# Two layers of attention and experts: for the first sequence only the two chosen experts of a token are computed, in gathered blocks, and in causal heads TensorE does the steps between heads in the middle of a batch

## The reference

```
logits = xf @ Wr + br
topk_w, topk_idx = top_k(logits, 2)
topk_w = softmax(topk_w)
gate = sum(one_hot(topk_idx, 8) * topk_w[..., None], axis=1)
h = relu(einsum('th,ehf->etf', xf, W1) + b1)        # 128 -> 256
y = einsum('etf,efh->eth', h, W2) + b2              # 256 -> 128
out = einsum('te,eth->th', gate, y)
```

## Time and profile before

| | |
|---|---|
| median of 3 runs | 1223.13 us (1223.12 to 1223.13) |
| profiled execution, its own time | 1223.02 us |
| its span, first to last instruction | 1221.2 us |
| TensorE / VectorE / ScalarE / GpSimd busy | 91% / 71% / 64% / 23% |
| heads of layer 0 | to 307.5 us |
| experts 0 | 307.5 to 446.6 us |
| heads of layers 1 and 2 | 446.6 to 1089.4 us |
| experts 1 | 1089.4 to 1211 us |

### The profile page before, as it was taken

The page is one execution under the profiler, slowest core; times in us unless marked ns, Lnnn a source line. Parts: engine busy times, 40 slices in busy tenths (PEclk is TensorE's granted clock), DMA queues, the critical chain, the costliest instruction groups (busy, mean ns, idle before and its releaser), DMA issues. The chain is left out here.

```text
span 1221.2 us, 24980 instructions
## 1 busy us (share of the span) xinstructions
PE 1105.6 (91%) x8797; PEld 605.1 (50%) x8872; DVE 864.5 (71%) x2072; ACT 777.3 (64%) x1569; POOL 281.8 (23%) x824
## 2 busy tenths in 40 slices
PE   5899998999999989999988999788888988899996
PEld 3466676655776755666655642222112221137774
DVE  3788767784334467888776889899999989904433
ACT  4366656667444426677666658878888878874443
POOL 8134322333102113433332431111101010100001
PEclk9799999999999999999999999999999989999998
DMA  3444343110000801243312221101111100000000
GB/s 88 118 115 109 96 96 87 49 31 12 1 1 1 184 10 32 59 105 94 85 49 65 55 43 36 24 16 24 36 36 36 23 11 16 7 1 1 10 9 18
DMA packets 40058, 57.71 MB, mean 47 GB/s; under 512 B 9494, under 2 KB 15078, under 8 KB 39678
## 3 DMA queue, kind: packets, MB, share of 16 engines
q1 hardware_dynamic: 39934, 56.11, 18.8%
HBM read 30.81 MB, written 24.64 MB: 45 GB/s over the span
## 5 line engine op out<-in xcount | busy, mean ns | idle before, releaser
L851 ACT ACTIVATE probs<-bank 128x512 f32<-128x512 f32 x1088 | 574.9, 601 | 240.8 <-PE bank L1210 239.8
L950 DVE TENSOR_REDUCE tile_max<-bank 128x1 f32<-128x512 f32 (+3 forms) x1152 | 611.9, 592 | 40.2 <-PE bank L1195 35.6
L1195 PE MATMUL bank<-qk 125*128 125x128 bf16 (+2 forms) x1664 | 389.1, 312 | 66.8 <-DVE tile_max L950 47.0
L1210 PE MATMUL bank<-qk 128*128 128x128 bf16 (+4 forms) x1608 | 362.6, 305 | 5.7 <-ACT probs L851 5.3
L1239 PE MATMUL bank<-probs,v_head 128*32 128x512 f32 (+3 forms) x3328 | 302.9, 453 | 0.1
L1195 PEld LDWEIGHTS bank<-qk 125*128 125x128 bf16 (+1 forms) x1664 | 132.4, 97 | 313.7 <-DVE tile_max L950 243.0
L1117 DVE SCALAR_TENSOR_TENSOR acc<-bank,gate,acc 128x128 f32<-128x128 f32 x256 | 71.9, 343 | 156.7 <-PE bank L1372 156.7
L1239 PEld LDWEIGHTS bank<-probs,v_head 128*32 128x32 f32 x3328 | 139.6, 109 | 52.7 <-issue 29.8
L1210 PEld LDWEIGHTS bank<-qk 128*128 128x128 bf16 (+1 forms) x1664 | 133.1, 97 | 57.2 <-ACT probs L851 21.0
L871 ACT ACTIVATE probs<-bank,sb_b 128x512 f32<-128x512 f32 x128 | 81.0, 684 | 117.9 <-PE bank L1361 117.9
L944 DVE TENSOR_REDUCE tile_max<-bank 128x4 f32<-128x512 f32 x128 | 87.4, 687 | 90.0 <-PE bank L1195 89.9
(11 more groups left out here) (132 smaller groups left out, 664.2 us busy)
## 6 DMA issues: line engine op xcount, KB each, us to landing
qk<-qk_parts SPq DMA_DIRECT2D x160, 144.0 KB
qk_parts<-q_parts SPq DMA_DIRECT2D x48, 192.0 KB, 2.4
qk_parts<-k_parts SPq DMA_DIRECT2D x48, 192.0 KB, 3.2
qk_parts<-q_parts SPq DMA_DIRECT2D x24, 96.0 KB, 2.3
qk_parts<-k_parts SPq DMA_DIRECT2D x24, 96.0 KB, 2.9
sb_w<-in_w SPq DMA_DIRECT2D x8, 256.0 KB, 3.6
sb_w<-in_w SPq DMA_DIRECT2D x2, 1024.0 KB, 5.2
qk<-neg_rows SPq DMA_DIRECT2D x96, 6.0 KB
```

The source lines that it names most:

```text
L851: nc.scalar.activation(probs[:, hd.probs_place(c), :], S2[i % len(S2)][:], ACT.Exp, scale=hd.a.scale).then_inc(sem("probs"), 1)
L950: ins = nc.vector.tensor_reduce(tile_max[:, hd.slot, t, which:which + 1], s1[:, at:at + P * count], AX.X, ALU.max)
L1195: ins = mm(s1[:, at:at + P * count], qk[hd.query_rows, hd.place, 0, P * t:P * (t + 1)], qk[hd.query_rows, hd.place, 1, P * k0:P * (k0 + co ...
L1210: ins = mm(s2[:, at:at + P * count], qk[hd.key_rows, hd.place, 1, P * j:P * (j + 1)], qk[hd.key_rows, hd.place, 0, P * q0:P * (q0 + count) ...
```

## The change

For sequence 0 of each mixture, once routing has picked two experts for each token, every pair of token and expert gets a slot in a list that is sorted by expert, where each expert begins on a multiple of 128. There are at most 23 blocks of 128 slots (`BLOCKS`). GpSimd writes each token's row to its two slots in DRAM (`x_blocks`, 16 indirect DMAs of 128 rows, step `scatter`), SP loads the blocks back (`blocks`), TensorE turns them (step `gx`, VectorE copies to `xgT`), and six block units of up to four blocks (`BLOCK_UNITS`) take the place of 16 dense ones: `UNITS` is 22, of which the last 16 are the dense units of sequence 1. Since the expert of a block is only known on the chip, SP reads it to a register and loads the block's weights, 256 KB, from `w_blocks`, where DMAs have put W1 and W2 of an expert side by side. 14 or 18 blocks are loaded in the last heads, to memory that is free there (weights of the other stretch, parts of sequence 0, `a_tok`, `x_plus`), the rest at the end. ScalarE makes `hidden` block by block, since the bias differs. VectorE copies `Y` out, SP stores it to `y_blocks`, GpSimd gathers each token's two rows (16 indirect DMAs, step `gather`), and VectorE adds them with their weights (step `combine`).

Four places (`IN_FRONT`) stand ahead of `up(0)` of a stretch. The gate sums (`gateT`, `gb`) of sequence 0 move from the heads into the stretch. In causal heads TensorE now does a place's steps behind the second chunk of the next batch, as in non-causal ones, and ScalarE and VectorE read a chunk later. The beginning has nine more small instructions of GpSimd for constants.

```diff
+BLOCKS = (TOP * S + E * (P - 1)) // P
+BLOCK_UNITS = -(-BLOCKS // TPC)
+PRELOADED = 18
+UNITS = BLOCK_UNITS + CB * E
+IN_FRONT = 4
...
+first = at_unit(0, -1, 0)
+put(first, ("biases", 0))
+for m, i in enumerate((0, 1, 5, 7, 9, 11)):
+    put(later(first, i), ("gx", 0, m))
+put_attention_out(0, 1, first, (2, 3, 4, 6, 8, 9, 10, 12, 13, 14))
+put_routing(0, 1, first, (14, 15, 15, 16, 16))
+put_gate_sums(0, 1, first, (17, 18, 26, 27))
+put_gate_sums(0, 0, first, (19, 20, 21, 22))
+for c, i in enumerate((24, 29)):
+    put(later(first, 17), ("gather", 0, c))
+    put(later(first, i), ("combine", 0, c))
...
+            def blocks(f):
+                sp.wait_ge(sem("scattered"), 16 * TOP * TB * (f + 1))
+                for m in range(BLOCK_UNITS):
+                    n = len(blocks_of(m))
+                    sp.dma_start(xg[m][:, 0:P * n].rearrange("p (j d) -> p j d", d=D),
+                                 x_blocks[f].rearrange("(j p) d -> p j d", p=P)[:, TPC * m:TPC * m + n, :]
+                                 ).then_inc(sem(f"x_in{m}"), 16)
+                for j in range(PRELOADS[f][0], PRELOADED, 4):
+                    preload(f, range(j, min(j + 4, PRELOADED)))
+                sp.wait_ge(sem("pv"), BATCHES[RUNS[f].stop])
+                load_block_weights(f, range(PRELOADED, BLOCKS))
...
+            def scatter(f, i):
+
+                t = i % TB
+                pool.wait_ge(sem("slots"), f + 1)
+                pool.wait_ge(sem("cleared"), 16 * BLOCKS * (f + 1))
+                if f == 1:
+                    taken(pool, "mtok", t // TPC)
+                tokens_of = (x, x_plus)[f]
+                nc.gpsimd.indirect_dma_start(x_blocks[f], bass.IndirectOffsetOnAxis(ap=places[:, i:i + 1], axis=0),
+                                             tokens_of[:, t, :], None).then_inc(sem("scattered"), 16)
+
+            def gather(f, c):
+
+                pool.wait_ge(sem("pv"), BATCHES[RUNS[f].stop])
+                for m in range(2):
+                    pool.wait_ge(sem(f"y_stored{m}"), 16 * BLOCK_UNITS // 2 * (f + 1))
...
             def experts(f, last):
+                normalise(last)
+                for i in range(IN_FRONT):
+                    between(at_unit(f, -1, i))
+                dve.wait_ge(sem("out"), last + 1)
...
-                        if c == batch[1] and before is not None and not HEADS[before[1]].a.causal:
+                        if c == batch[1] and before is not None:
                             between(before)
...
-                    if hd.a.causal:
-                        between(at_head(g, k))
...
                 loaded(pe, f"ffn{f}")
                 pe.wait_ge(sem("max_taken"), CHUNKS[RUNS[f].stop])
+                turn_sums(last)
+                for i in range(IN_FRONT):
+                    between(at_unit(f, -1, i))
                 up(0)
-                turn_sums(last)
```

More of the change, by code:

```diff
@@ L206, in put_attention_out, with put_routing, put_gate_sums, put_places_of_tokens @@
     return at[9]
-def put_routing(f, b, place, at=range(9)):
-    c0, c1 = BY_SEQUENCE[b]
-    for i, step in zip(at, (("logits", f, b), ("route_top", f, b), ("route_exp", f, b), ("route_weights", f, b),
-                            ("route_gate", f, b), ("gateT", f, c0), ("gateT", f, c1), ("gb", f, c0), ("gb", f, c1))):
-        put(later(place, i), step)
+def put_routing(f, b, place, at):
+    for i, step in zip(at, ("logits", "route_top", "route_exp", "route_weights", "route_gate")):
+        put(later(place, i), (step, f, b))
+def put_gate_sums(f, b, place, at=range(4)):
+    for i, step in zip(at, [(kind, f, c) for c in BY_SEQUENCE[b] for kind in ("gateT", "gb")]):
+        put(later(place, i), step)
+def put_places_of_tokens(f, place, at, each):
+    for i, step in zip(at, ("ranks", "slots", "blocks")):
+        put(later(place, i), (step, f))
+    for i in range(TOP * TB):
+        put(later(place, at[1] + 1 + int(i / each)), ("scatter", f, i))
 def put_qkv(L, c, place, offsets=range(4)):
@@ L373, in build @@
         gateT = aT[0:E, :]
+        zeros = sb("zeros", [P, D])
+        weighted = sb("weighted", [P, TOP, TB, E])
+        chosen = sb("chosen", [P, TB + 1, E], BF16)
+        ranks = sb("ranks", [P, TB + 1, E])
+        counted = sb("counted", [P, 5, E])
+        tables = sb("tables", [P, BLOCKS, E])
+        block_at_i = sb("block_at_i", [P, BLOCKS], I32)
+        block_at = sb("block_at", [P, BLOCKS])
+        expert = sb("expert", [P, BLOCKS])
+        expert_i = sb("expert_i", [P, BLOCKS], I32)
+        b1_blocks = sb("b1_blocks", [P, FB, BLOCKS])
+        places_f = sb("places_f", [P, TOP, TB])
+        places = sb("places", [P, TOP * TB], U32)
+        earlier16 = sb("earlier16", [P, P], BF16)
+        ones16 = sb("ones16", [P, P], BF16)
+        before128 = sb("before128", [P, E, E])
+        xg = [part[:, i, S:T].bitcast(F32) for part in parts for i in range(PARTS)]
+        xgT = [rest[:, i, :] for i in range(2)]
+        y_out = sums
+        yg = probs[:, 4:8, :].rearrange("p a (t d) -> p (a t) d", d=D)
         iota_i = sb("iota_i", [P, E], I32)
@@ L644, in between @@
                         route_gate(*which)
+                    if kind == "scatter":
+                        scatter(*which)
+                    if kind == "gather":
+                        gather(*which)
             def route_gate(f, b):
@@ L731, in _ @@
                 add_quarters(GROUP[run.stop - 1])
-                for m in range(UNITS):
-                    for half in range(2):
-                        between(at_unit(f, m, half))
+                between(later(at_unit(f, -1, 0), -1))
+                for place in units_places(f):
+                    between(place)
         @block.scalar
@@ L790, in between @@
                         nc.scalar.activation(xT[:, tokens(which[1])], SHARED[:], ACT.Copy).then_inc(sem("taken"), 1)
+                    if kind == "mtok":
+                        full(act, step)
+                        nc.scalar.activation(x_plus[:, tiles(which[0]), :],
+                                             SHARED[:].rearrange("p (t d) -> p t d", d=D), ACT.Copy
+                                             ).then_inc(sem("taken"), 1)
                     if kind == "eff":
@@ L853, in head @@
                         before = at_place_before(run, g, k)
-                        if c == batch[hd.read_after] and before is not None:
+                        if c == batch[2] and before is not None:
                             between(before)
@@ new lines, in combine @@
+            def combine(f, c):
+                dve.wait_ge(sem(f"gathered{c}"), 16 * TOP * TPC * (f + 1))
+                taken(dve, "gb", f, c)
+                for i in range(TOP):
+                    for t in range(TPC * c, TPC * (c + 1)):
+                        ins = nc.vector.scalar_tensor_tensor(acc[:, t, :], yg[:, TB * i + t, :], small[:, 1 + i, t:t + 1],
+                                                             acc[:, t, :], ALU.mult, ALU.add)
+                    if i == 0:
+                        link(ins)
+                ins.then_inc(sem("combined"), 1)
@@ L1092, in between @@
                         route_weights(*which)
+                    if kind == "ranks":
+                        take_ranks(step)
+                    if kind == "blocks":
+                        block_of(*which)
+                    if kind == "slots":
+                        slots(*which)
+                    if kind == "biases":
+                        biases(*which)
+                    if kind == "combine":
+                        combine(*which)
+                    if kind == "gx":
+                        f, m = which
+                        n = P * len(blocks_of(m))
+                        full(dve, step)
+                        if m >= 2:
+                            dve.wait_ge(sem("hid_ps"), UNITS * f + m - 1)
+                        nc.vector.tensor_copy(xgT[m % 2][:, 0:n], SHARED[:, 0:n]).then_inc(sem("taken"), 1)
                     if kind == "v":
```

300 lines of the change are left out of this document (245 added, 55 removed).

## The result

The changed kernel took 1243.64 us (median of 4 runs, 1238.71 to 1246.69) where the kernel before took 1223.13: a ratio of 1.0163, with an interval of 1.0126 to 1.0200. In these runs it is slower, by 1.3 to 2.0%, and my prediction of 1196 us (1178 to 1214) was wrong.

What follows compares the result with a forecast made beforehand. TensorE was taken to bound the expert stretches, VectorE the non-causal heads. Terms: -66.1 + 9.7 + 24.0 + 3.0 + 4.0 + 1.0 - 3.0 = -27.4 us, giving 1196 us, range 1178 to 1214.

Steps and rivals of the forecast that it cites:

- the pricing of GpSimd's indirect DMAs: Scatters and gathers: GpSimd's time for one bounded by 0.3 and 1.28 us times two, taken as 1.2.
- the rival on the slower side: Gathers behind units 6 to 12, scatters in layer 0's heads: slow indirect DMAs make the change end slower; chance 0.10.
- The lock: In the stretches, GpSimd locked while VectorE adds gathered rows: 16 instructions of 0.34 us, 5.5 a stretch; chance 0.05.
- the rival *between: Gathers of 1.3 to 1.8 us, or GpSimd locked during VectorE's adds: 1207 us, with both up to 1220; chance 0.13.
- the causal order: Causal heads: TensorE's step moves behind the next batch's second chunk, some waits go, others grow; -3.0 us, bounds -12 and +3.
- the half clock: Behind each front, some 4.6 us at the lower clock of 1.2 GHz, so 2.3 us lost at each.
- The saving of work: Expert stretches: 16 dense units go, 23 blocks and their transposes come; -33.0 us a stretch, -66.1 in all.
- the fronts: Ahead of `up(0)`: first waits for GpSimd's last scatter and the load, second for VectorE's biases; +24.0 us with half clock.
- The waits for turned tokens: At `gx` 2 to 5, `up` waits for VectorE's copies: 1.2 us idle, four times a stretch, +9.7 us in all.
- The heads: Heads outside the stretches: VectorE's bookkeeping +4.0 us in layer 2 and +1.0 in layer 0, causal order -3.0.
- the 4.0 of my sum: Layer 2's heads, where VectorE idles 2.6%: its new bookkeeping of 17 instructions makes them +4.0 us longer.
- Loads of weights: Last heads: the 18 and 14 early weight loads stay hidden, priced at nothing; otherwise 3.6 us in a head.

Runs made afterwards that it cites:

- the execution with the delay: Profile of the changed kernel as first run, when ScalarE and VectorE started late beside the gathers; those runs took 1243.64 us against 1223.13 before.
- the repeat without the delay: The changed kernel run again, nothing edited, in another set (kernels run one after another on one chip): 1209.95 us, ratio 0.9879 to the kernel before.
- third set: Changed kernel again, 1243.34 us; with turning of tokens one place earlier, 1236.54; with denser scatters and biases moved into heads, 1241.11; with both moves, 1233.48.
- The run with the new order alone: The kernel before with only the changed order of steps in the causal heads: 1219.44 us, ratio 0.9968.
- fourth set: Told together with a fifth: changed kernel with half the gathers, or plain loads for gathers, or mixes by stretch; five kernels, 1205.28 to 1208.23 us.
- the seventh: Changed kernel with earlier turning and relieved fronts, plus GpSimd waiting for eight gathers to land before the next eight: 1215.55 us; without that pause 1233.65.
- sixth set: Changed kernel with earlier turning and relieved fronts, 1235.19 us; changed kernel with half the gathers in the first stretch, GpSimd's plain loads in the second, 1214.60.

## Why the prediction was wrong

**The step that failed** is the pricing of GpSimd's indirect DMAs. I bounded GpSimd's own time for one, took 1.2 us, found "up to 1.3 us a gather is free" and stopped there; the rival on the slower side needed g = 1.84. Measured is a pace of 1.25 us, close to what I took, in sets of both kinds. The cost is elsewhere: ScalarE and VectorE start late while a row of them is under way. By parts, the execution with the delay against the one without: heads of layer 0 +3.8 us, first stretch +12.8, heads of layers 1 and 2 -0.9, second stretch +13.1; in the spans 1236.8 against 1208.0, in the medians 33.7 us. I had no term, no rival and no bound for a delay of engines that have nothing to do with the DMA. "Slower" had its chance of 0.10 for a reason that did not occur. Nor was the rest of the sum right: without the delay the time lies in my range, but only half of the gain is there, as the parts below show.

**The lock** of the rival *between*. The Trainium skill ("SBUF — State Buffer", section "SBUF: two separate sides") has VectorE with two SBUF inputs and a GpSimd instruction that reads SBUF exclude each other for one instruction, and says that ScalarE waits on nobody there. My prediction tied the waiting descriptors to that case too; that section of the Trainium skill tells of them for VectorE's two-port modes. The traces show that the lock is not the cause. In the repeat without the delay, the gathers beside VectorE's adds of two SBUF tensors (383.72 to 386.02) last 0.95 us, like those without them. In the result VectorE does nothing at all from 376.28 to 392.91, so there it shuts nobody out, and a wait of 16.64 us, or ScalarE's of 7.98, is no single instruction of GpSimd's.

**The rest of the sum, without the delay.** The profiled repeat (span 1208.0) is 14.2 us above my 1193.8 (1221.2 - 27.4). Cut into the four parts, with my terms in the same cut (the gate sums of layer 0, 3.0, leave its heads for the first stretch; of the causal order I give 1.0 to layer 0 and 2.0 to layer 1):

| part | forecast | measured |
|---|---|---|
| heads of layer 0 | -3.0 | +0.5 |
| first stretch | -10.8 | -6.5 |
| heads of layers 1 and 2 | +2.0 | +5.8 |
| second stretch | -15.6 | -13.0 |

Its stretches in the windows view:

```profile
305.40:440.80 135.40, 111.62 (x715) 85.61 (x716) 51.90 (x195) 57.56 (x131) 40.01 (x55) 0.95 0.32 90
1086.70:1208.00 121.30, 98.83 (x624) 74.81 (x624) 47.34 (x178) 52.11 (x115) 23.69 (x36) 0.93 0.14 41
```

TensorE's idle time in them grew by 17.4 and 12.0 us over the kernel before; my waits and fronts, less the half clock in them, made 16.9 and 12.1. Its busy time fell by 23.8 and 25.0; I had 27.7 (33.0 less the gate sums and 2.3 at half clock). So the sums of the waits agree within 0.5 us, but that is partly luck: the waits that I had named come to some 14.4 and 10.5 us, and waits that I had not named grew by the rest, 3.0 and 1.5 us. The saving of work was 4 and 3 us too high. Of the first, 1.3 is a longer half clock (see the fronts below); the rest was not traced.

**The waits for turned tokens**: four of 1.2 us forecast, 0.97 to 1.04 measured in the first stretch and 0.83 to 0.99 in the second, 4.0 and 3.7 us in place of 4.8. The view names ScalarE's `probs` or nothing as their end, but each time TensorE starts 0.1 us after VectorE's copy of the tokens has ended (345.40 and 345.50), so the releaser is the one that I had. When they were taken away (third set), 6.8 us came back of 7.7.

**The fronts**: right in their place and their causes, and 1 us short in size. From the last head's multiply to `up(0)` it took 15.2 and 11.0 us, where I had 14.3 and 9.6. In the set without the delay TensorE waited 6.95 us for the load from `x_blocks`, behind the last scatter, and in the second stretch 3.59 us for VectorE's biases:

```profile
318.07 1.12 PE L1648 MATMUL bank<-ident,q_parts 128*128 128x128 f32 x4 [6.95 <-DMA q_parts<-x_blocks]
320.06 1.09 PE L1648 MATMUL bank<-ident,q_parts 128*128 128x128 f32 x4 [0.88 <-DVE rest L1390]
...
324.77 5.21 PE L1691 MATMUL bank<-rest,sb_w 128*128 128x128 f32 x32
```

The half clock began earlier than I had it, ahead of the first transposes (0.50 in 316 to 324): 3.6 us lost in the first front, where I took 2.3. That is in the three rows: groups of four transposes at 1.1 us, not 0.63, and an `up` at 5.2 us, not 3.6.

**The heads**: too low by 3.5 and 3.8 us. The run with the new order alone is the base to hold them against. Its heads of layer 0 end at 303.85 us, those of the changed kernel at 305.40, though the gate sums have left them: +1.6 where my other terms make -2.0. That `ranks`, the scatters and VectorE's bookkeeping filled the place is my reading, not shown. The heads of layers 1 and 2 take 637.4 us with the new order alone and 645.9 in the changed kernel. Of these 8.5 us, 3.9 come between the starts of `load_max` at 953 and 1008 us, where routing and its new bookkeeping stand (970 to 1001 us): that is the 4.0 of my sum. The other 4.6 come earlier, in the last heads of layer 1 and the first of layer 2, where I had no term; what they are was not followed.

**The causal order**: -3.0 forecast, -3.9 measured, by itself. This term was right, and it was the widest bound that I had.

**Loads of weights**, priced at nothing: TensorE never waits for `w_blocks` in either kind of set. Right.

## What stays open

What makes a set one with the delay. It is not the program: the changed kernel has both kinds, and so has the kernel with half the gathers, then plain loads. It is not the chip's number: chips 9, 10 and 11 showed no delay and chip 2 did, twice, but chip 5 showed none in the fourth set and the delay in the seventh. Within each of the eight sets (the result's is one), all kernels with scatters are of the same kind. The core, its neighbours or the state of the chip may differ from set to set; nothing in these traces tells them apart.

How the indirect DMAs delay the two engines is also open. What the rows make unlikely: longer transfers, for the gathers' packets take nearly the same time in both kinds, 18.2 and 17.3% of it. The DMA view over the 22.2 us from the first gather's start, with the delay:

```profile
q0 software_dynamic: 512, 1.05, 18.2%
...
probs<-y_blocks,places POOLq DMA_INDIRECT x16
```

and without:

```profile
q0 software_dynamic: 512, 1.05, 17.3%
...
probs<-y_blocks,places POOLq DMA_INDIRECT x16, 2.5
```

The packets and bytes are equal; but with the delay the trace finds no landing for a gather (the 2.5 us is missing), as it finds no releaser for the waits. That would fit signals that arrive late or out of their order, not late data, but it is an argument, not shown, and one view speaks against leaning on it: in the sixth set the 16 plain loads, which delayed nobody, have no landing either, where they have one of 2.2 us in sets without the delay. Code loading does not fit either: the Trainium skill ("Runtime: NRT & Kernel Launch", section "Instruction fetch mechanics") has code fetched by DMA in blocks; in the trace only two such packets fall into these 22.2 us, both before 378, and the longest waits end at 392.9. Whether the scatters do the same for the same reason was not tried by itself; the head at their end is 2.6 us longer or more (9.87 against 7.31) in every set with the delay. Why a short wait in the row helps so much is open with the rest.

## What to carry to other kernels

Price an indirect DMA of GpSimd not only by GpSimd's time but by what the other engines do beside it: with no rows for it, a rival "the others start late while it runs" is worth its chance. Issue such DMAs in short rows with a wait for their landing between them where there is slack: here, in a set with the delay, 2.3 us of waiting were worth 9 us in each stretch; what it costs in a set without was not measured. And before an experiment that takes a cost away is believed, run the unchanged kernel beside it in the same set; a part of the kernel that the edit does not touch (here a head with scatters) can serve as the sign.

## What the hardware showed that I had not expected

- Sixteen indirect DMAs in a row held ScalarE up for 8.0 us and VectorE for 16.6 us at a time; eight held ScalarE up for 3.4 us; sixteen plain ones of the same queue and size, issued in 8.6 us, nobody.
- In the first stretch ScalarE's first late start came 7.16, 7.13 and 7.17 us after the first gather's start, in kernels with sixteen, eight, and eight with a pause. In the second stretch of the result, where other steps stand beside the gathers, it came after 12.2 us.
- GpSimd takes the same time for scatters and gathers: 0.94 to 1.0 us (the first of a row up to 1.1), and 0.30 us between two that follow each other at once. Sixteen plain DMAs of 64 KB take it 8.6 us, 0.54 each.
- The kernel before, which has no such DMA, took the same time in all eight sets (medians 1223.1 to 1224.0).
